# Own work lists for the last two turns, with part of the expert mixing moved to VectorE

## What is computed

```python
h = _layernorm(x) * (1 + ca) + sa
x = x + ga * attention(h)
h = _layernorm(x) * (1 + cb) + sb
# product keys: two sets of 64 scores for each head, top 8 of the sums, softmax over them
w = silu(h @ down_embed[idx].T) * softmax(scores)
mlp = (silu(h @ Wg + bg) * (h @ Wu + bu)) @ Wd + bd
x = x + gb * (mlp + sum(w * up_embed[idx]))
```

## Time and profile before

| what | value |
|---|---|
| time, median of 3 runs | 1511.75 us (1511.45 to 1513.72) |
| profiled execution, its own time | 1514.42 us |
| its span (first to last instruction) | 1512.6 us |
| PE busy | 1405.7 us (93%) |
| DVE busy | 1356.1 us (90%) |
| ACT busy | 1242.2 us (82%) |
| POOL busy | 1082.9 us (72%) |

### The profile page before, as it was taken

How to read it: one execution, slowest core, us unless ns; L and a number is a source line. 1 busy time by engine, 2 the same in 40 slices (tenths; PEclk the granted TensorE clock), 3 DMA queues, 4 the chain that set the end, 5 groups by cost and what they waited for, 6 DMA issues and landing times.

```text
span 1512.6 us, 39371 instructions
## 1 busy us (share of the span) xinstructions
PE 1405.7 (93%) x11361; PEld 1151.4 (76%) x11361; DVE 1356.1 (90%) x5366; ACT 1242.2 (82%) x4103; POOL 1082.9 (72%) x1201
## 2 busy tenths in 40 slices
PE   3789999999999999999999999999999999999963
PEld 2567888887788887778888777887887788788742
DVE  5579999999999999999999999999999999999853
ACT  1788888988888898888889888888988888888831
POOL 2017877777787777778777777877777787777786
PEclk7999999999999999999999999999999999999976
DMA  5000000000000000000000000000000000000000
GB/s 129 15 13 6 20 20 19 16 19 14 9 19 19 19 16 19 14 9 19 19 19 16 19 14 9 19 19 19 16 19 14 9 19 19 19 16 12 13 8 7
DMA packets 50880, 27.86 MB, mean 18 GB/s; under 512 B 10304, under 2 KB 50048, under 8 KB 50848
## 3 DMA queue, kind: packets, MB, share of 16 engines
q1 hardware_dynamic: 50608, 27.05, 6.9%
q10 hardware_dynamic: 240, 0.43, 0.1%
HBM read 23.15 MB, written 4.31 MB: 18 GB/s over the span
## 4 chain that ended last, share of the span: by engine, by line
PE 60%; DVE 25%; issue 5%; ACT 5%; POOL 3%; DMA 1%; DVEq 0%; POOLq 0%; ACTq 0%
PE pS L1054 9%; PE pW L996 9%; PE pW L998 7%; PE pW L997 7%; PE pW L1067 6%; PE pS L1044 5%; DVE pS L764 5%; DVE h L862 5%; PE pS L1040 4%; ACT pS L534 4%; PE pW L1128 4%; PE pW L1131 4%; PE pW L1071 2%; DVE p_sb L784 2%; PE pW L1119 2%
## 5 line engine op out<-in xcount | busy, mean ns | idle before, releaser
L534 ACT ACTIVATE pS<-pS,nmx 128x128 f32<-128x128 f32 (+1 forms) x1024 | 390.4, 441 | 53.7 <-DVE nmx L764 53.7
L427 POOL TENSOR_TENSOR fexp<-fexp,fsum 128x512 f32<-128x512 f32 x256 | 320.6, 1283 | 80.6 <-DVE fexp L900 80.6
L764 DVE CUSTOM_DVE_ANT_0 pS<-pS,mask 128x128 f32<-128x128 f32 (+1 forms) x1024 | 330.1, 390 | 23.3 <-PE pS L1044 22.8
L418 POOL TENSOR_TENSOR fsum<-ex 128x512 f32<-128x512 f32 x256 | 257.6, 1043 | 0.0
L526 ACT COPY pT<-pS 128x768 f32<-128x768 f32 x256 | 211.7, 827 | 36.0 <-PE pS L1054 31.5
L1054 PE MATMUL pS<-ident,p_sb 128*128 128x128 f32 x1536 | 216.3, 277 | 10.4 <-DVE p_sb L784 6.5
L784 DVE TENSOR_TENSOR p_sb<-pS,coef 128x256 f32<-128x256 f32 (+2 forms) x512 | 210.5, 453 | 8.9
L1054 PEld LDWEIGHTS pS<-ident,p_sb 128*128 128x128 f32 x1536 | 173.3, 141 | 41.5 <-issue 13.5
L534 ACT ACTIVATION_READ_ACCUMULATOR pS<-pS,nmx 128x1 f32 x1024 | 202.2, 197 | 0.0
L434 POOL TENSOR_TENSOR fexp<-fexp 128x512 f32<-128x512 f32 x128 | 172.1, 1364 | 0.2
L516 ACT COPY qk<-pW 128x512 f32<-128x512 f32 x256 | 166.7, 651 | 6.0 <-PE pW L998 6.0
(11 more groups left out here) (164 smaller groups left out, 3642.0 us busy)
## 6 DMA issues: line engine op xcount, KB each, us to landing
x_in<-in_L_attn_tokens SPq DMA_DIRECT2D x32, 128.0 KB, 2.1
modA<-mods_dram SPq DMA_DIRECT2D x32, 128.0 KB, 3.1
x_res<-in_L_attn_tokens SPq DMA_DIRECT2D x32, 128.0 KB, 3.0
modB<-mods_dram SPq DMA_DIRECT2D x32, 128.0 KB, 2.9
out<-yo SPq DMA_DIRECT2D x32, 128.0 KB, 1.9
modC<-mods_dram SPq DMA_DIRECT2D x32, 64.0 KB, 3.0
fsum<-in_L_attn_Wkv SPq DMA_DIRECT2D x2, 512.0 KB, 6.5
fsum<-in_L_attn_Wq SPq DMA_DIRECT2D x1, 512.0 KB, 4.7
```

The source lines that it names most:

```text
L418: ins = nc.gpsimd.tensor_tensor(fsum[:, k, h], ex[:, k, h, 0:NX].unsqueeze(2).broadcast_to([P, NX, NK]), ex[:, k, RH + h, :].unsqueeze(1). ...
L427: ins = nc.gpsimd.tensor_tensor(fexp[:, k, h, :], fexp[:, k, h, :], fsum[:, k, h].rearrange("p i j -> p (i j)"), ALU.mult)
L534: ins = nc.scalar.activation(ps, ps, ACT.Exp, bias=nmx[:, p % 2, h, k:k + 1], scale=-1.0, accum_out=den(p)[:, h, k:k + 1])
L764: ins = nc.vector.tensor_tensor_reduce(out=ps, in0=ps, in1=mask[:, (1 - k) * P:2 * P], scale=-1.0, scalar=LARGEST, op0=ALU.add, op1=ALU.mi ...
```

## The change

Turns 32 and 33 get lists of their own on GpSimd, ScalarE and VectorE; all other turns and TensorE's list stay as they are. GpSimd no longer does block 0 of the experts in these turns: VectorE makes its products (`products`), its choice (`select`, one instruction that compares `fsum` with the threshold and multiplies by it) and its head sum (`sum_heads`, which puts `rz` in). In turn 33 it does so for `select` and `sum_heads` of block 1 too, so that GpSimd has only `products(1)` and both `fold` left. GpSimd's `add_bias` comes first in turn 32. Each step of the new VectorE helpers waits for the one before it (`select_next`). `junk` gets one row for each block. ScalarE's `total` calls move behind those of the gates.

```diff
-        junk = sb("junk", [P, NE])
+        junk = sb("junk", [P, TB, NE])
...
+        select_link, fold_link = sem("select_link"), sem("fold_link")
...
 # GpSimd
                 def weigh(k):
                     if w.live(-2):
-                        pool.wait_ge(S(masks_ready), at(masks_ready, g, k + 1))
+                        pool.wait_ge(S(masks_ready), at(masks_ready, g, 1 if last else k + 1))
...
+                if last and i == B:
+                    add_bias()
+                    candidates()
+                    products(1)
+                    weigh(1)
+                    rstd2()
+                    add_heads(1)
+                    fold(1)
+                    fold(0)
+                    return
+                if last:
+                    candidates()
+                    products(1)
+                    add_bias()
+                    fold(0)
+                    fold(1)
+                    return
...
 # ScalarE
+                if isinstance(i, int) and i == B:
+                    copy_transposes(7, -1)
+                    weighted(6)
+                    gate_up(1)
+                    down_tanh(0)
+                    weighted(7)
+                    down_tanh(1)
+                    gate_up(2)
+                    gate_up(3)
+                    modulate_h()
+                    high_part(h2T_high, h2T, "hT")
+                    total(1)
+                    expert_exp(0)
+                    total(0)
+                    expert_exp(1)
+                    experts(0)
+                    experts(1)
+                    gate_up(0)
+                    return
+                if isinstance(i, int) and i > B:
+                    gate_up(1)
+                    down_tanh(0)
+                    down_tanh(1)
+                    gate_up(2)
+                    gate_up(3)
+                    total(0)
+                    experts(0)
+                    total(1)
+                    experts(1)
+                    return
...
 # VectorE
+                def select_next(ins):
+
+                    links[0] += 1
+                    ins.then_inc(select_link, 1)
+                    dve.wait_ge(select_link, links[0])
+
+                def products(k):
+                    dve.wait_ge(S(tops_ready), at(tops_ready, g, 1))
+                    dve.wait_ge(S(eo_ready[k]), at(eo_ready[k], g - 1, 1))
+                    for h in range(RH):
+                        ins = nc.vector.tensor_tensor(fsum[:, k, h], ex[:, k, h, 0:NX].unsqueeze(2).broadcast_to([P, NX, NK]),
+                                                      ex[:, k, RH + h, :].unsqueeze(1).broadcast_to([P, NX, NK]), ALU.mult)
+                    select_next(ins)
+
+                def select(k):
+                    if k == 1:
+                        dve.wait_ge(S(f_ready[k]), at(f_ready[k], g, 1))
+                        dve.wait_ge(S(eo_ready[k]), at(eo_ready[k], g - 1, 1))
+                    for h in range(RH):
+                        row = fsum[:, k, h].rearrange("p i j -> p (i j)")
+                        ins = nc.vector.scalar_tensor_tensor(out=fexp[:, k, h, :], in0=row, scalar=top8[:, k, h, TK - 1:TK], in1=row,
+                                                             op0=ALU.is_ge, op1=ALU.mult)
+                    select_next(ins)
+
+                def sum_heads(k):
+                    dve.wait_ge(S(rz_ready), at(rz_ready, g, 1))
+                    select_next(nc.vector.tensor_scalar(wsum[:, k, :], fexp[:, k, 0, :], rz[:, k, 0:1], None, ALU.mult))
+                    for h in range(1, RH):
+                        ins = nc.vector.scalar_tensor_tensor(out=wsum[:, k, :], in0=fexp[:, k, h, :], scalar=rz[:, k, h:h + 1], in1=wsum[:, k, :],
+                                                             op0=ALU.mult, op1=ALU.add)
+                        if h < RH - 1:
+                            select_next(ins)
+                    ins.then_inc(S(wsum_ready[k]), 1)
...
+                if isinstance(i, int) and i == B:
+                    products(0)
+                    thresholds()
+                    bias_product(1)
+                    gate_product(1)
+                    gated_down(0)
+                    choose(1, 0)
+                    choose(1, 1)
+                    gated_down(1)
+                    bias_product(2)
+                    gate_product(2)
+                    ln2_stats()
+                    bias_product(3)
+                    gate_product(3)
+                    ln2_modulate()
+                    select(0)
+                    low_part(h2T_high, h2T, "hT")
+                    shift(0)
+                    sum_heads(0)
+                    shift(1)
+                    finish()
+                    bias_product(0)
+                    gate_product(0)
+                    return
+                if isinstance(i, int) and i > B:
+                    products(0)
+                    bias_product(1)
+                    gate_product(1)
+                    thresholds()
+                    select(0)
+                    sum_heads(0)
+                    select(1)
+                    sum_heads(1)
+                    gated_down(0)
+                    bias_product(2)
+                    gate_product(2)
+                    gated_down(1)
+                    bias_product(3)
+                    gate_product(3)
+                    finish()
+                    return
```

More of the change, by code:

```diff
@@ L395, in split_weights @@
                 ins.then_inc(const_pool, 1)
+            folds = [0]
             def body(i):
@@ L399, in body @@
                 f, g = i - 1, i - 2
+                last = isinstance(i, int) and i >= B
                 def candidates():
@@ L443, in fold @@
                         nc.gpsimd.tensor_scalar(wsum[:, k, NE - 1:NE], wsum[:, k, NE - 1:NE], tot[:, k:k + 1], float(RH),
-                                                ALU.subtract, ALU.add).then_inc(S(pool_sum[k]), 1)
-                        pool.wait_ge(S(pool_sum[k]), at(pool_sum[k], g, 3))
+                                                ALU.subtract, ALU.add).then_inc(fold_link if last else S(pool_sum[k]), 1)
+                        if last:
+                            folds[0] += 1
+                            pool.wait_ge(fold_link, folds[0])
+                        else:
+                            pool.wait_ge(S(pool_sum[k]), at(pool_sum[k], g, 3))
                         w.wait_released("D", k, g)
@@ L589, in total @@
                         act.wait_ge(S(wsum_ready[k]), at(wsum_ready[k], g, 1))
-                        nc.scalar.activation(junk[:, :], wsum[:, k, :], ACT.Copy, accum_out=tot[:, k:k + 1]).then_inc(S(tot_ready[k]), 1)
+                        nc.scalar.activation(junk[:, k, :], wsum[:, k, :], ACT.Copy, accum_out=tot[:, k:k + 1]).then_inc(S(tot_ready[k]), 1)
                 def rms_scale():
@@ L751, in scale_weights @@
                 nc.vector.tensor_scalar(b_gh[:, :], b_g[:, :], 0.5, None, ALU.mult).then_inc(const_dve, 1)
+            links = [0]
             def body(i):
@@ L895, in choose @@
                     if w.live(-2):
-                        if k == 0 and half == 0:
+                        if (k == 0 or isinstance(i, int) and i >= B) and half == 0:
                             dve.wait_ge(S(rz_ready), at(rz_ready, g, 1))
```

## The result

The changed kernel takes 1517.16 us (median of 8 runs, 1515.21 to 1518.63). The kernel before takes 1512.15 on the same chip (8 runs, 1511.45 to 1514.45). The forecast was +3.4 us (+0.22%). As a time it was 1515.2; the median itself lies 0.3 us over the upper end of the range, the ratio put on the median of before (1511.75 x 1.0027 = 1515.8) lies inside it. The profiled execution has a span of 1516.0 us, 3.4 over the 1512.6 of before.

A forecast was written before the change was run, and what follows sets the result against it. GpSimd was taken to bound both turns. Turn 32's +5.3 and turn 33's -1.9 us summed to +3.4, put on the median 1511.75: 1515.15 us (+0.22%), range 1510.6 to 1516.9.

The forecast's parts named there:

- Step 1: Turn 32, to the addition of modB (L844): early x2g removes 2.85 us of waiting, late gate brings 3.0 back; +0.2.
- the first rival: TensorE's clock falls earlier in turn 32, output projection up to 5.3 us; step 1 +1.8, total +4.5 to +5; chance 0.17.
- Step 2: Turn 32, to hT: gate_product(3) ends at 1455.0, then two h take 1.5 us; sum so far -0.9.
- Step 3: Turn 32, select(0) ahead of low_part on VectorE: about 3.9 us beside GpSimd, 2.7 alone; sum so far +0.85.
- Step 4: Turn 32, similarity(0) to transpose_experts(0): 9.05 us instead of 5.1, as block 0 becomes the last; sum so far +4.8.
- Step 5: Turn 32, to gate_product(0): 10.45 us as before, plus 0.5 for project_ffn at the low clock; sum so far +5.3.
- Turn 33: To the last transpose_experts: VectorE's serial list of 15.6 us plus 10.0 behind it, 25.6 against 27.45 before; -1.9.
- The last of the prediction's three signs of being wrong: The prediction is wrong if TensorE's granted clock in the last 60 us isn't that of before.
- no blocking: Turn 32's products run side by side on VectorE and GpSimd: step 1 loses 2.8 us, total about -1.4; chance 0.10.
- That instructions with all data in SBUF are faster: VectorE's 21 unblocked instructions near 0.54 us, not 0.68: 0.14 less each, -3, total about +0.4; chance 0.06.

The follow-up runs named there:

- e2: Changed kernel with the new lists only in turn 32, turn 33 as before the change: ratio 1.0041 to the kernel before.
- e10: Changed kernel with short filler transposes added on TensorE where it waits in the last two turns: ratio 0.9990 to the kernel before.
- e5: Changed kernel with turn 33 reordered: gate_product(1) and gated_down(0) ahead of thresholds, selections and sums, ScalarE's experts(0) behind total(1): ratio 1.0002 to the kernel before.
- e6: Changed kernel with sum_heads(0) of turn 32 taking one head, three of its four instructions left out: ratio 1.0013 to the kernel before.
- Experiment 1: Changed kernel with the new lists only in turn 33, turn 32 as before the change: 1510.50 us against 1513.09 for the kernel before, ratio 0.9981.
- e3: Changed kernel with GpSimd's products(1) of turn 32 waiting until VectorE's products are done: ratio 1.0002 to the kernel before.
- e4: Changed kernel with GpSimd's products(1) of turn 32 replaced by memsets of the same tiles: ratio 0.9996 to the kernel before.
- e9: Filler transposes on TensorE, added to reordered lists where VectorE takes only turn 33's selections and sums: ratio 0.9934 to the kernel before, 0.9921 without fillers.

## Why the prediction was right, step by step

Starts in us after G, and the difference to before. The run with turn 32 alone (e2) has the same lists up to the end of that turn.

| step | before, us after G | after, us after G | predicted difference | difference, after | difference, e2 | difference, e10 |
|---|---|---|---|---|---|---|
| 1, `modB` added (L844) | 12.49 | 14.43 | +0.2 | +1.94 | +0.37 | +0.36 |
| 2, `hT` | 19.48 | 19.98 | -0.9 | +0.50 | -0.99 | -1.01 |
| 3, `similarity(0)` | 21.75 | 24.19 | +0.85 | +2.44 | +0.95 | +0.95 |
| 4, `transpose_experts(0)` | 26.85 | 33.16 | +4.8 | +6.31 | +4.82 | +4.14 |
| 5, `gate_product(0)` | 36.88 | 43.17 | +5.3 | +6.29 | +4.47 | +3.32 |
| turn 33 to the last transposes | 27.89 | 25.85 | -1.9 | -2.04 | -0.17 | -2.09 |
| from there to the last `yo` | 7.69 | 7.00 | 0 | -0.69 | -0.14 | -2.53 |

(The predicted differences of steps 1 to 5 are the sums so far. The last two rows are lengths, the first of them from the start of `gate_product(0)`. e2 has the old turn 33, and e10 is the changed kernel with the clock held over most of the tail.)

- **Step 1** failed in the profiled execution, and held where the clock did. The blocked products were right to 0.02 us (5.32 against 5.3), GpSimd's too (5.39), `x2g` came at 1435.47 and nothing waited for `modB`. The gate ended at 1445.17 against 1445.25. But the granted clock is at its lower level (1.2 GHz) from 1439.0 to 1442.4 and from 1445.8 to 1449.2. The first of these stretches isn't the late gate's doing: it begins behind a wait of 1.94 us for `p_sb`, which the kernel before has too, at full clock (TensorE's timeline):
```profile
1437.83 0.85 PE L1054 MATMUL pS<-ident,p_sb 128*128 128x128 f32 x6 [1.94 <-ACT p_sb L541]
```
VectorE reached its gate without a wait all the same, so it cost nothing there; it only shortened TensorE's wait for that gate to 1.77 us, from the 3.30 of e2, e5 and e6. The second stretch begins just behind that wait, and it is what costs: the output projection takes 4.58 us instead of 3.73, and `modB` is added 1.94 later, not 0.2 (0.85 by the projection, the rest by the matmuls ahead of it, 2.24 us from `project_down(1)` to the projection against 1.51, and by the difference in G). That is the first rival, with its place and nearly its price (+1.8). It is not the same in every execution: with the same lists up to there, and the longer wait, the projection took 3.73 us in e2, 5.00 in e5 and 5.23 in e6.
- **Step 2** rested on `h` in 1.5 us (1.81 measured) behind a `gate_product(3)` ending at 1455.0 (1455.95, with the late step 1). From L844 to `hT` it is 5.55 us, against 6.99 before: -1.44 where -1.1 was said; the matmuls of `gate_up(3)` ran at full clock in 1.0 us, not in 1.7.
- **Step 3**: `select(0)` took 3.74 against 3.9, blocked by GpSimd's heads and `fold`, whose own `wsum` and `fold` grew from 1.26 to 1.79 and 1.54.
- **Step 4**, the largest term, was right to 0.1: from `similarity(0)` to `transpose_experts(0)` 8.97 us against 9.05 predicted. `sum_heads` is 2.83 (0.48 to start with, 2.32, one overlap) for 2.85. Experiment 6 shows that it lies on the path.
- **Step 5**: no +0.5 by the clock in that stretch: 10.01 us against 10.03 before. The clock's loss came earlier, in step 1, and was three times as large. In e2 and e10 this stretch is 0.35 and 0.8 us shorter than before.
- **Turn 33**: 25.4 us from the end of the gate to the last transposes, against 25.6: a serial list of 15.6 (1481.26 to 1496.91) and 9.9 behind it. Experiment 1 shows the -2 alone.
- **Not foreseen**: the last stretch is 0.69 shorter. Its clock was low for 3.9 us of the 7.0 instead of 5.3 of 7.7.

So the sum, 3.4, met the tail's 3.57 with errors that cancel: turn 32 ends 6.29 late where 5.3 was said (the clock, in step 1 instead of 5), turn 33 gives 0.14 more back, and the end 0.69. VectorE's and GpSimd's terms were each met within 0.3 us; that the total fits to 0.2 us is luck, for it hangs on where the clock fell in this execution. The last of the prediction's three signs of being wrong did come up: over the last 60 us of the tail the granted clock is at its low level for 41.0 us, where before it is for 47.4, and 10 us earlier it is low where before it is full (0.71 against 1.00 in 1440 to 1450 us).

In e2, whose clock held until 16.1 us after G, steps 1 to 4 are met within 0.2 us. The rival *no blocking* was wrong, by 5.32 and 5.39 us for four products, but its arithmetic wasn't: with the products apart (e3) L844 comes 2.47 sooner, where -2.5 was said. That instructions with all data in SBUF are faster is refuted by 0.68 for a product; one that reads its scalar from a tile takes 0.75. One reading of the rows was off without a consequence: L878 is slow in 29 of its 32 turns, not in 31 (0.28 us in the first one and in turns 31 and 32).

The Trainium skill's rule on the two engines (SBUF — State Buffer, "Who interferes with whom") holds for this pair: apart (e3) both have their own price again, and beside a GpSimd that only writes (e4) VectorE has. The blocking is nearly full here, a pair every 1.45 us against 1.60 one after the other. The Trainium skill's rule that the clock drops after idle (TensorE: Matmul & The Clock Gate, "What's actually happening") was given 0.17. The drop is in the traces of the changed kernel, e5 and e6, and not in that of e2, whose wait was as long.

## What to carry to other kernels

Work that is handed to a second engine is worth what that engine is waited for at that moment. Here it was worth 6.6 us for selection and sums in turn 33, with GpSimd done with its products (10.4 with the lists reordered too), and it cost 4.2 us for products and block 0's sums in turn 32, where VectorE's gate is what TensorE waits for and GpSimd reads beside it. Before moving anything between VectorE and GpSimd, look at whether both will read SBUF in the same stretch; if they must, let the one that is waited for go first and make the other wait. And where a move leaves TensorE idle just ahead of a long run of matmuls, price that run at both clocks.

## What the runs showed of the chip

- A VectorE `tensor_tensor` of 128x512 (0.68 us alone) and a GpSimd one (1.04 alone) that read SBUF beside each other: 1.53 and 1.49 each, a pair starting every 1.45 us. Alone VectorE's follow each other every 0.60 and GpSimd's every 1.00 us: 1.60 one after the other, so side by side gains a tenth. A GpSimd memset (0.53) beside the same VectorE instruction slows neither. Single instructions collide too: a VectorE sum of 0.75 us took 1.64 beside a GpSimd `fold`, itself 1.65 instead of 1.26 (e9).
- The granted clock in a wait-ridden stretch differs between executions of the same instruction lists: it first fell 1.2, 6.0, 8.8 and 16.1 us after G (the changed kernel, e5, e6, e2), and the projection took 4.58, 5.00, 5.23 and 3.73 us. TensorE waited at the same places in them. A profile shows one such draw; a term of this kind should be given as a range.
- Idle time of TensorE filled with small transposes kept the clock up and gained 2.1 us in one kernel, 4.9 in another and none in a third: in the third GpSimd's `fold` and VectorE's sums came last ahead of the last transposes, and the added transposes held TensorE themselves.
